# Spreading 128 recurrence units over 48 expert tiles, in half-of-states order, with GpSimd's products after the sort

## The reference, cut to what matters

```
# layer 0 mixture: 2048 tokens, 16 experts, width 192, top 2
h = silu(x @ gate_w[e]) * (x @ up_w[e]);  out += weight * (h @ down_w[e])
# layer 1 recurrence: 4 sequences, 512 channels d, 16 states n, 512 steps t
state[d,n] = state[d,n] * exp(dt[d] * A[d,n]) + dt[d] * u[d] * B[n]
y[d] = sum_n state[d,n] * C[n] + D[d] * u[d];  y = y * silu(z)
```

## Time and profile before

| | us |
|---|---|
| median of three runs | 1670.61 |
| the profiled execution's own time | 1678.16 |
| its span, first to last instruction | 1676.4 |
| DVE scan of the first unit | 304.48 |
| slot_tok | 318.55 |
| first scan inside tile 0 | 427.15 |
| last read-out of the recurrence | 829.62 |
| PE, DVE, ACT, POOL busy | 1411.9, 957.4, 679.1, 752.2 |

### The profile page before, as it was taken

One profiled execution on the slowest core, in us unless ns is written; L12 is line 12 of the kernel. 1 busy time (PEld: TensorE's weight loads), 2 busy tenths in 40 slices (PEclk: granted clock), 3 DMA queues, 4 the chain that ended last, 5 costly groups with the idle time before them and its releaser, 6 DMA issues.

```text
span 1676.4 us, 19321 instructions
## 1 busy us (share of the span) xinstructions
PE 1411.9 (84%) x6048; PEld 1046.9 (62%) x6048; DVE 957.4 (57%) x1234; ACT 679.1 (41%) x1239; POOL 752.2 (45%) x559
## 2 busy tenths in 40 slices
PE   6988981545798789789727699999999999999998
PEld 3534540535465556456517588787878787878786
DVE  2667768899799689789868313233242424242422
ACT  4345442244465455456414333333333333333332
POOL 0000004266677468568363244445454545454543
PEclk9798895556899899889955599999999999999999
DMA  3211225005668787977575680001000100010000
GB/s 100 102 39 62 102 77 225 29 0 191 229 206 258 270 267 242 314 252 240 168 220 189 246 293 13 0 0 63 13 0 0 63 0 13 0 50 0 0 0 25
DMA packets 76465, 191.18 MB, mean 114 GB/s; under 512 B 10664, under 2 KB 15560, under 8 KB 74880
## 3 DMA queue, kind: packets, MB, share of 16 engines
q1 hardware_dynamic: 63104, 157.03, 27.8%
q0 software_dynamic: 6400, 20.98, 4.2%
q10 hardware_dynamic: 6912, 12.59, 2.0%
HBM read 152.55 MB, written 38.01 MB: 114 GB/s over the span
## 4 chain that ended last, share of the span: by engine, by line
PE 63%; DVE 17%; DMA 8%; issue 7%; ACT 2%; SPq 2%; POOL 1%; ACTq 0%; DVEq 0%; POOLq 0%
PE decay L1668 21%; PE bank L1657 20%; DVE decay L1211 8%; DMA WGU<-in_L_ffn_up_w 6%; PE bank L1540 5%; PE bank L1515 2%; PE bank L1456 2%; PE bank L1558 2%; PE decay L1412 2%; DVE XH L1077 1%; PE bank L1419 1%; PE bank L1476 1%; PE decay L1466 1%; PE decay L1462 1%; PE bank L1498 1%
## 5 line engine op out<-in xcount | busy, mean ns | idle before, releaser
L1369 DVE CAST HFH<-HF 128x512 fp32r<-128x512 f32 x128 | 58.9, 460 | 497.3 <-ACT HF L1008 497.3
L693 POOL TENSOR_TENSOR S<-DTU,Bb 128x1024 f32<-128x1024 f32 x128 | 299.6, 2362 | 68.0 <-PE bank L1515 50.5
L784 POOL TENSOR_TENSOR W2L<-W2R,W2H 128x512 fp32r<-128x512 f32 x128 | 172.3, 1346 | 348.9 <-ACT W2H L1003 348.9
L1211 DVE TENSOR_TENSOR_SCAN decay<-decay,S 128x1024 f32<-128x1024 f32 x128 | 292.9, 2288 | 1.5 <-ACT decay L861 1.5
L1657 PE MATMUL bank<-XSH,W1H 128*128 128x512 f32 x512 | 203.1, 397 | 4.2 <-POOL W1L L780 4.2
L1668 PE MATMUL decay<-W2H,HFH 128*128 128x512 f32 x512 | 200.4, 391 | 5.3 <-DVE HFL L1371 5.3
L1657 PE MATMUL bank<-XSH,W1L 128*128 128x512 f32 x512 | 203.0, 397 | 0.0
L1657 PE MATMUL bank<-XSL,W1H 128*128 128x512 f32 x512 | 202.6, 396 | 0.0
L1668 PE MATMUL decay<-W2L,HFH 128*128 128x512 f32 x512 | 199.9, 391 | 0.0
L1668 PE MATMUL decay<-W2H,HFL 128*128 128x512 f32 x512 | 199.6, 390 | 0.0
L1540 PE MATMUL bank<-WGU,XGT 128*128 128x384 f32 x384 | 151.1, 542 | 51.1 <-DMA WGU<-in_L_ffn_up_w 50.4
(11 more groups left out here) (208 smaller groups left out, 2079.0 us busy)
## 6 DMA issues: line engine op xcount, KB each, us to landing
WGU<-in_L_ffn_gate_w SPq DMA_DIRECT2D x48, 384.0 KB
WGU<-in_L_ffn_up_w SPq DMA_DIRECT2D x48, 384.0 KB
WD<-in_L_ffn_down_w SPq DMA_DIRECT2D x48, 384.0 KB, 3.9
Bb<-bc_rows SPq DMA_DIRECT2D x32, 512.0 KB, 7.5
Cb<-bc_rows SPq DMA_DIRECT2D x32, 512.0 KB, 8.5
expert_rows<-YT ACTq DMA_DIRECT2D x48, 256.0 KB
W1R<-in_L_ffn_w SPq DMA_DIRECT2D x6, 1024.0 KB, 13.5
W2R<-in_L_ffn_w SPq DMA_DIRECT2D x6, 1024.0 KB, 14.4
```

Of the source, the lines that this page charges most:

```text
L693: pool.tensor_tensor(S[j][:], DTU[:, ds(b, 1), c, :].to_broadcast([P, PAIR, L]), Bb[j][:], ALU.mult).then_inc(dbu_ready, 1)
L784: pool.tensor_tensor(W2L[f % 2][:], W2R[:, ds(e, 1), f, :].rearrange("p e d -> p (e d)"), W2H[f % 2][:].bitcast(F32), ALU.subtract).then_i ...
L1211: dve.tensor_tensor_scan(flat, flat, S[j][:].rearrange("p i l -> p (i l)"), 0.0, ALU.mult, ALU.add).then_inc(scan_done, 1)
```

## The change: what it does

- `place(u)` gives a new order of the 32 units of a sequence: first the state pairs 0 to 3 for all four channel groups, then 4 to 7. A group of YS now has four units, and a sequence eight groups.
- The result of a first-half group goes into U (whose skip term is in it by then), and PE adds it back with one matmul by the identity at the end of the second-half group.
- Six units (AHEAD) run before the tiles. The other 122 are spread over the 48 tiles by `cuts`, two or three each, and all loops over sequences become written-out code.
- SP issues the loads of row pairs by `rows_of(j)`, behind the weights of tile j + 1, once their last unit lies in an earlier tile; U comes in four loads of 256 KB instead of one of 1 MB.
- POOL waits for `hot_ready` of at least 1 (`row_hot` done) before its first product.
- DA buffers go by u % 2 and S buffers by u % 8.

```diff
+    HP = NP // 2
+    GB = 2 * DC
+    def place(u):
+        return u // (UB // 2), u // HP % DC, u // (UB // 2) * HP + u % HP
+        AHEAD = 6
+        ALL = B * UB
+        cuts = [AHEAD + (ALL - AHEAD) * j // SLOT_TILES for j in range(SLOT_TILES + 1)]
+        def split(j):
+            us = units(j)
+            ends = [i + 1 for i, u in enumerate(us) if u % HP == HP - 1 and i + 1 < len(us)]
+            at = ends[0] if ends else (len(us) + 1) // 2
+            return us[:at], us[at:], bool(ends)
...
 SP
+            def last_use(j):
+                return j // HP * (UB // 2) + (DC - 1) * HP + j % HP + 1
-                    sp.wait_ge(dbu_ready, b * UB + (j + 1 - NP))
+                    sp.wait_ge(dbu_ready, b * UB + (last_use(j) - UB))
+            def load_u(b, c):
+                if not isinstance(b, int) or b:
+                    sp.wait_ge(s_summed, b * UB + ((c + 1) * HP - UB // 2))
+            def rows_of(j):
+                lo, hi = (cuts[j - 1] if j else 0), cuts[j]
+                for b in range(1, B):
+                    for p in range(NP):
+                        if lo < (b - 1) * UB + last_use(p) <= hi:
+                            load_b(b, p)
+                            load_c(b, p)
+                    for c in range(DC):
+                        if lo < (b - 1) * UB + UB // 2 + (c + 2) * HP <= hi:
+                            load_u(b, c)
+            for j in range(SLOT_TILES):
+                if j + 1 < SLOT_TILES:
+                    load_expert(0, j + 1)
+                rows_of(j)
...
 POOL
-            for c in range(DC):
-                for j in range(NP):
-                    dbu(0, c, j)
+            pool.wait_ge(hot_ready, 1)
+            for u in range(AHEAD):
+                dbu(0, u)
             pool.wait_ge(slots_ready, 1)
             gather(0, 0)
             gather(0, 1)
+            for j in range(SLOT_TILES):
+                for u in units(j):
+                    dbu(*bu(u))
+                if j + 2 < SLOT_TILES:
+                    gather(0, j + 2)
...
 ACT
+            def take_y(b, g):
+                c = g % DC
+                wait_apart(act, s_summed, b * UB + (g + 1) * HP)
+                if g < DC:
+                    act.copy(U[:, c, :], YS[:]).then_inc(y_ready, 1)
+                else:
+                    act.copy(DTU[:, ds(b, 1), c, :].rearrange("p b l -> p (b l)"), YS[:]).then_inc(y_ready, 1)
+            for j in range(SLOT_TILES):
+                ds_ = units(j)[1:] + units(j + 1)[:1]
+                decay(*bu(ds_[0]))
+                copy_ht(0, j)
+                if j > 1 and units(j - 2)[-1] % HP == HP - 1:
+                    take(units(j - 2)[-1])
+                if j:
+                    copy_y(0, j - 1)
+                    store_y(0, j - 1)
+                if j + 1 < SLOT_TILES:
+                    tanh_g(0, j + 1)
+                first, _, ends = split(j - 1)
+                if ends:
+                    take(first[-1])
+                if ds_[1:]:
+                    decay(*bu(ds_[1]))
+                if j + 2 < SLOT_TILES:
+                    copy_xg(0, j + 2)
+                scales(units(j))
+                for u in ds_[2:]:
+                    decay(*bu(u))
...
 DVE
+            for j in range(SLOT_TILES):
+                for i, u in enumerate(units(j)):
+                    scan(*bu(u))
+                    if i == 1 and j + 1 < SLOT_TILES:
+                        gate_h(0, j + 1)
+                    read_out(*bu(u))
+                    if i == 1 and j + 1 < SLOT_TILES:
+                        finish_h(0, j + 1)
...
 PE
+                elif i0 == HP - 1:
+                    ins = pe.matmul(YS[:], ident[:], U[:, c, :], start=False, stop=True, skip_group_check=True)
-            for u in range(UB - 2):
+            for u in range(HP):
                 add_states(0, u)
+            for j in range(SLOT_TILES):
+                first, rest, _ = split(j - 1)
+                turn_h(0, j, j == SLOT_TILES - 1)
+                if j + 1 < SLOT_TILES:
+                    up(0, j + 1)
+                for u in first:
+                    add_states(*bu(u))
+                if j + 2 < SLOT_TILES:
+                    turn_x(0, j + 2)
+                for u in rest:
+                    add_states(*bu(u))
+                down(0, j)
```

More of the change, by code:

```diff
@@ L331, in build_program @@
         cb_loaded = [sem(f"cb_loaded{j}") for j in range(NP)]
-        ul_loaded = sem("ul_loaded")
+        ul_loaded = [sem(f"ul_loaded{c}") for c in range(DC)]
         da_ready = sem("da_ready")
@@ L437, in build_program, with units, bu @@
         NAT_LOADS, SMALL_LOADS = 3, 11
+        AHEAD = 6
+        ALL = B * UB
+        cuts = [AHEAD + (ALL - AHEAD) * j // SLOT_TILES for j in range(SLOT_TILES + 1)]
+        def units(j):
+            return list(range(HP, AHEAD)) if j < 0 else list(range(cuts[j], cuts[j + 1])) if j < SLOT_TILES else []
+        def split(j):
[3 more added lines that the diff above has]
+            return us[:at], us[at:], bool(ends)
+        def bu(u):
+            return u // UB, u % UB
         block = top.enter_context(nc.Block())
@@ L523, in _ @@
                 load_c(0, j)
-            load_u(0)
+                if j < DC:
+                    load_u(0, j)
             sp.wait_ge(tex_ready, 1)
             sp.wait_ge(slots_ready, 1)
[L528 to L549, removed]
-            load_expert(0, 0)
[L552 to L558, removed]
+            def rows_of(j):
[8 more added lines that the diff above has]
+                            load_u(b, c)
+            load_expert(0, 0)
+            for j in range(SLOT_TILES):
+                if j + 1 < SLOT_TILES:
+                    load_expert(0, j + 1)
+                rows_of(j)
             def load_x1(b):
@@ L910, in _ @@
             act.sem_inc(yt_stored, DMA)
[L912 to L938, removed]
@@ L940, in _ @@
             copy_xg(0, 0)
+            take(HP - 1)
+            decay(0, AHEAD - 1)
             tanh_g(0, 0)
             copy_xg(0, 1)
[L943 to L947, removed]
+            decay(0, AHEAD)
+            for j in range(SLOT_TILES):
[19 more added lines that the diff above has]
+                    decay(*bu(u))
@@ L949, in silu_z @@
+            copy_y(0, SLOT_TILES - 1)
+            store_y(0, SLOT_TILES - 1)
+            for u in units(SLOT_TILES - 2)[-1:] + units(SLOT_TILES - 1):
+                if u % HP == HP - 1:
+                    take(u)
             def silu_z(b):
@@ L1232, in finish_h @@
                                          ALU.mult).then_inc(hh_ready, 1)
-            for u in range(UB):
+            for u in range(AHEAD):
                 scan(0, u)
@@ L1593, in _ @@
             turn_x(0, 1)
-            with pe.Fori(1, B - 1) as b:
-                mixture_steps(b, False)
-            mixture_steps(B - 1, True)
-            add_states(B - 1, UB - 2)
-            add_states(B - 1, UB - 1)
+            for j in range(SLOT_TILES):
[10 more added lines that the diff above has]
+                down(0, j)
+            for u in units(SLOT_TILES - 1):
+                add_states(*bu(u))
             def turn_gated(b):
```

123 lines of the change are left out of this document (36 added, 87 removed).

## The result

The changed kernel takes 1659.76 us (median of 6 runs, 1657.10 to 1665.07), against 1670.08 us for the kernel before (6 runs, 1667.17 to 1675.28). The ratio is 0.9939, interval 0.9922 to 0.9956: faster by 0.6%, 10 us. The forecast was 1632.1 us, 38 us less. The time lies inside the widest range stated (1605 to 1662), near its upper end, and outside the forecast's own (1618 to 1650); the gain is about a quarter of the one forecast.

The account below looks back on a forecast made before the run. The prediction took DVE's work to bound the recurrence and expert tiles: tiles start at 332.3, DVE's 440.0 and stalls of 18 + 2 end at 792.3, 38.5 us earlier. So 1670.6 - 38.5 = 1632.1 us, range 1618 to 1650.

Parts of the forecast that it names:

- The sort: Sort on DVE: without GpSimd's products beside it 12.4 us are freed; tile_hot beside products gives back 7.0.
- Start of the tiles: From slot_tok to the first scan inside tile 0: tiles start at 332.3 us, units 4 and 5 fitting under it.
- The tiles' own work: Dense-expert tiles: 122 units plus gating take DVE 440.0 us, 9.2 a tile; work of PE, ACT and GpSimd is hidden.
- rival (4): Tiles: single YS bank and later decays couple ACT, PE and DVE; 0.8 us lost per tile, about 1671 us; chance 0.04.
- rival (3): Tiles: PE falls to the slow clock level and becomes the bound; slower, 12 such tiles give 1706 us; chance 0.08.
- Stalls: Tiles: six bursts of row loads, 4.2 MB each, cost 3 us each, 18 in all, between 0 and 48.
- rival (2): Tiles: bursts of row loads cost as before, 8 us each, 30 more, 1662 us; chance 0.15.
- the prediction's own sign of being wrong: Tiles: the forecast is wrong if PE's waits for gate/up weights (WGU) stay near 50 us, against about 20 expected.
- The mean rate: Tiles: about 105 MB over some 460 us is 229 GB/s, near the 223 that an undisturbed window carried.
- The sum: Whole kernel: last read-out moves from 830.8 to 792.3 us, 38.5 less, and what follows shifts with it.

Follow-up runs that it names:

- e4_hot3: The changed kernel with GpSimd's first product waiting for the whole sort, row_hot and both pairs of tile_hot: 1650.34 us, ratio 0.9891 to the kernel before.
- e1_spread: The changed kernel with at most one pair of row loads behind the weights of each tile, same bytes: 1641.37 us, ratio 0.9852 to the kernel before.
- e3_small_rows: The changed kernel with row reloads of sequences 1 to 3 cut to 4 KB, leaving out part of the computation: 1614.99 us, ratio 0.9677.
- e6_all: The changed kernel with one row pair a tile at most, gate/up weights issued ahead of rows, and GpSimd behind the whole sort: 1607.74 us, ratio 0.9636.
- e2_wgu_first: The changed kernel with gate and up weights of tile j+2 issued on SP ahead of the rows behind tile j: 1629.38 us, ratio 0.9760.
- e5_before_wait: The kernel before with only GpSimd's wait for row_hot added: 1662.76 us, ratio 0.9970.
- e7_old_order: The changed kernel with the old order of states and groups of eight, even spread and sort wait kept: 1653.59 us, ratio 0.9914.

## Why the prediction was wrong

The direction, the place of the gain and most terms held.

- **The sort.** Forecast 12.4 us freed and 7.0 given back, 5.4 net; slot_tok moved by 52.8 - 46.5 = 6.3 us, 12.6 freed and 6.3 given back. OH and PSEL came to 0.76 instead of the 0.84 taken, and tile_hot grew by 6.3, not 7.0. Three products got in between, as the pattern of PSEL had shown for one. The Trainium skill (GPSIMD Engine Reference, section Specifications) names DVE instructions with two SBUF inputs as contending with GpSimd for SBUF; this trace agrees (9.95 us against 3.65), and e4_hot3 confirms it by taking the two apart (3.64 us).
- **Start of the tiles.** Forecast 332.3 on the time base of before, measured 65.7 + 265.8 = 331.5. That units 4 and 5 fit under the chain was almost right: unit 5 waited 2.70 us for its decay, which ACT had queued behind a copy, without effect on the first scan of the tiles, for the tanh came later still. That 331.5 comes so close is in part luck: the path was priced with PE at its slow level, and PE was there in the execution profiled (four transposes in 1.06 us at 316.10). In e1_spread, with the same stream up to there, they took 0.64 and the first scan came 3.3 us earlier, at 62.4 after the start of the sort.
- **The tiles' own work.** Forecast 440.0; e3_small_rows took 442.7, e6_all 442.8. Alternating tiles of 7.31 and 10.77 us are there. PE, ACT, GpSimd and the one bank YS are hidden in these two, as costed; in the change decays that come late behind stalls, each with a copy of YS ahead of it on ACT, take 8.1 us of the 46.0, which the prediction had only in its rival (4). The clock in the stretch is 0.93 in the change, so rival (3) did not come.
- **Stalls: the step that failed.** The prediction took "3 us x 6 = 18", plus 2 for the start. Measured: 46.0 us in all and 2.7 without the rows, so 43.3 / 6 = 7.2 us a burst, near the upper bound of 8. This misses 26 us, and the last read-out stood at 551.7 + 265.8 = 817.5 us instead of 792.3. It is rival (2), 1662 us, which had 0.15, and the prediction's own sign of being wrong, WGU waits near 50 us, came with 55.1. The rate was not bad: 4.2 MB at 340 to 379 GB/s, and 409 measured. What was wrong is that spare time was added up over about three tiles, when the wait that ends last is one tile's weights. In the dearest burst they were behind 3.1 MB on one queue, in one tile; before's hand-made order had put at most 2.1 MB behind any tile. That is not the whole price: in the kernel before a tile whose weights were issued at 700.22, behind 2.1 MB and with as much behind the tile ahead of it, still lasted 10.2 us too long. And a stall adds to itself: the clock falls, gate/up take 4.75 instead of 2.75 us, and the queues run empty afterwards (74 GB/s). That rows ahead of one tile's weights carry the cost is shown by e1_spread and e2_wgu_first, each an edit that moves the same bytes (ratios 0.9852 and 0.9760 against 0.9939), and by e3_small_rows, where the rows are small. That the clock and the empty queues are part of each price is read from the traces and was not tested by itself.
- **The mean rate.** The argument that 229 GB/s lies near the 223 of an undisturbed stretch was true (220 measured, and 241 without stalls in e6_all) and said nothing about the time, because it is true of the average only.
- **The sum.** 38.5 forecast. In the two profiles 13.3 us were gained up to the last read-out: 38.5 less the 26.0 of the stalls, plus 0.8 of the start. The medians differ by 10.3. The execution of before that was profiled, from which the forecast and the 53.6 us of its loss come, was 8.1 us slower than its median, and e5_before_wait lost 48.4 us with the same tiles; so of the 7.6 us between 53.6 and 46.0 a part, or all, may be scatter.

So the change spends its new freedom in the wrong place. It stretches the way from last use to next use of a row from 8 to 20 units, and then issues the rows as early as it can, ahead of weights that are wanted much sooner.

What stays open: why the bursts of e7_old_order, with twice the bytes, cost only 12 us against 7.2, and why the third and the sixth burst of the change, alike in their pairs, cost 4.7 and 8.5. Runs with other numbers of pairs in neighbouring tiles would tell; they were not made.

## What to carry to other kernels

When a transfer with a late deadline and one with an early deadline share a queue, look at what stands in front of the early one in its own tile, not at the mean rate; issue the urgent one first and spread the other over its whole slack. Price a burst by the wait that it puts on the next needed buffer, with the lower clock that follows it. If one engine's short two-input instructions run beside GpSimd's long products, put the products behind the last of them, not behind most of them.

## What the runs showed of the hardware that was not expected

- Transfers on SP's queue keep their order closely enough for position to matter: moving 768 KB of weights in front of up to 3.1 MB took the loss from 46.0 to 20.3 us with the same issues otherwise.
- SP's issue itself can slow in a burst: row issues take 0.42 us each at first and 1.10 and 1.35 us for the fifth and sixth, so what is queued behind them is late before it is issued. It isn't always the last ones: in the same burst of e2_wgu_first the six took 0.42, 0.42, 0.76, 0.61, 0.48 and 0.51 us.
- GpSimd's product and DVE's two-input instruction take turns: between four instructions of 0.91 us came 2.1 us (one product) in the first pair and 4.2 us (two) in the second. GpSimd's six products took 16.66 us in the change and 13.89 in e4_hot3, so they too wait for DVE.
